# A graph network kernel: the radial and weight products of its second message stage read all 128 rows

## What is computed

```python
h = jax.nn.silu(radial_embedding @ W_r1 * RADIAL_DIM ** (-0.5))   # 8 radial values, W_r1 8 x 8
w = h @ W_r2 * RADIAL_DIM ** (-0.5)                               # W_r2 8 x 128
w_ss, w_vs, w_vt, w_st = jnp.split(w, 4, axis=1)
m_s = jnp.concatenate([ss * w_ss, m_s_tp * w_st], axis=1)
m_v = jnp.concatenate([vs * w_vs[:, :, None], m_v_tp * w_vt[:, :, None]], axis=1)
S = jax.ops.segment_sum(m_s, receivers, num_segments=n) * inv
V = jax.ops.segment_sum(m_v.reshape(m_v.shape[0], -1), receivers, num_segments=n) * inv
```

## Time and profile before

| | us |
|---|---|
| median of 3 runs | 19515.98 |
| lowest and highest run | 19462.58, 19540.44 |
| span of the profiled execution | 19527.8 |
| PE matmuls busy | 13705.4 (70%) |
| PE weight loads busy | 10208.8 (52%) |
| DVE busy | 11589.1 (59%) |
| POOL busy | 10499.0 (54%) |
| ACT busy | 4277.9 (22%) |
| first and last vy of edge2 start about | 12780, 15870 |

### The profile page before, as it was taken

The page is one execution under the profiler, slowest core; times in us unless marked ns, Lnnn a source line. Parts: engine busy times, 40 slices in busy tenths (PEclk is TensorE's granted clock), DMA queues, the critical chain, the costliest instruction groups (busy, mean ns, idle before and its releaser), DMA issues. The chain is left out here.

```text
span 19527.8 us, 364942 instructions
## 1 busy us (share of the span) xinstructions
PE 13705.4 (70%) x67902; PEld 10208.8 (52%) x67903; DVE 11589.1 (59%) x52990; ACT 4277.9 (22%) x11127; POOL 10499.0 (54%) x15826
## 2 busy tenths in 40 slices
PE   4467666766555557856888887689999974565555
PEld 2246666664333336745777766356666653333334
DVE  7778888885333336845665655267777754444443
ACT  7742222221111113422333332211111111000000
POOL 8878888886555553223555553045555522555560
PEclk9999999996555558978999999755555566555555
DMA  3011111111221115734555555011111110111121
GB/s 134 0 16 30 32 31 31 30 31 44 58 57 57 57 56 158 217 102 114 155 154 153 155 152 123 10 35 39 39 39 39 39 25 24 40 41 41 41 41 18
DMA packets 1925133, 1295.55 MB, mean 66 GB/s; under 512 B 1295114, under 2 KB 1679741, under 8 KB 1925096
## 3 DMA queue, kind: packets, MB, share of 16 engines
q1 hardware_dynamic: 1600808, 593.17, 13.5%
q0 software_dynamic: 324288, 701.98, 13.2%
HBM read 933.63 MB, written 367.36 MB: 67 GB/s over the span
## 5 line engine op out<-in xcount | busy, mean ns | idle before, releaser
L977 DVE TENSOR_TENSOR agg<-agg,edge_psA 128x256 f32 x4992 | 2078.2, 416 | 2042.1 <-issue 1567.3
L951 POOL DMA_INDIRECT edge_sv<-tab,edge_ix x1664 | 1569.1, 943 | 2169.6 <-DVE edge_ix L1332 1735.8
L951 POOL DMA_INDIRECT edge_xs<-tab,edge_ix x1664 | 1589.5, 955 | 1615.0 <-DVE edge_ix L1592 1141.0
L951 POOL DMA_INDIRECT edge_fs<-tab_a,edge_ix x1664 | 1573.0, 945 | 1634.7 <-DVE edge_ix L1044 1187.0
L1611 PE MATMUL edge_psA<-edge_oh,edge_xs 128*128 128x256 f32 x3328 | 1580.5, 626 | 1146.1 <-DVE agg L977 877.6
L610 POOL DMA_INDIRECT by_src<-send_row,send_pl x1664 | 1615.3, 971 | 1257.4 <-issue 1097.3
L662 PE MATMUL send_psX<-x_res,send_ohT 128*128 x3328 | 1315.5, 499 | 1188.2 <-ACT send_ohT L643 1078.8
L460 POOL DMA_INDIRECT records<-place_pl,place_place x1568 | 1614.4, 1030 | 550.9 <-issue 515.4
L1611 PEld LDWEIGHTS edge_psA<-edge_oh,edge_xs 128*128 128x128 f32 x3328 | 922.3, 306 | 1803.8 <-issue 935.1
L662 PEld LDWEIGHTS send_psX<-x_res,send_ohT 128*128 128x128 f32 x3328 | 833.9, 311 | 1758.4 <-issue 1758.4
L1398 PE MATMUL edge_psA<-edge_oh,edge_m 128*128 128x128 f32 x6656 | 1593.2, 421 | 0.7 <-DVE edge_m L1367 0.7
(11 more groups left out here) (310 smaller groups left out, 31165.4 us busy)
## 6 DMA issues: line engine op xcount, KB each, us to landing
edge_fd<-tab_b SPq DMA_DIRECT2D x1664, 128.0 KB
max_row<-by_src SPq DMA_DIRECT2D x392, 258.0 KB
running<-max_back POOLq DMA_DIRECT2D x392, 256.0 KB
records<-count_tmpl SPq DMA_DIRECT2D x64, 858.0 KB
send_pl<-records SPq DMA_DIRECT2D x832, 66.0 KB
edge_pl<-records SPq DMA_DIRECT2D x832, 50.0 KB
place_pl<-in_edge_attr SPq DMA_DIRECT2D x781, 50.0 KB
by_src<-send_row,send_pl POOLq DMA_INDIRECT x1664
```

Of the source, the lines that this page charges most:

```text
L951: pool.indirect_dma_start(rows[b % len(rows)][:, k, :], None, table[:], bass.IndirectOffsetOnAxis(ap=ix[b][:, k:k + 1], axis=0)).then_inc( ...
L977: v.tensor_tensor(block, block, psA[b % 2][:, k * 2 * D:(k + 1) * 2 * D], ALU.add).then_inc((s_half if k == 0 else s_acc)[b], 1)
```

## The change

The two products read all 128 rows of their operands. `rT` and `hr` (two buffers each) are cleared once at the start of the stage by four memsets on DVE, and ACT and PE wait for these before their first step. ACT still writes only the 24 and 16 rows in use. `wr1` and `wr2` were cleared over all rows before. So the rows below hold zeros in both operands and add nothing to the sums. No other instruction is added, removed or moved; every engine's order in the stage is the same.

```diff
--- before.py
+++ after.py
@@ -1285,7 +1285,7 @@
         psR = [ph.bank(f"psR{k}") for k in range(2)]
         psW = [ph.bank(f"psW{k}") for k in range(2)]
         psA = [ph.bank(f"psA{k}") for k in range(2)]
-        s_w, s_turn, s_zero, s_c, s_go = (ph.sem(n) for n in ("s_w", "s_turn", "s_zero", "s_c", "s_go"))
+        s_w, s_turn, s_zero, s_c, s_go, s_rows = (ph.sem(n) for n in ("s_w", "s_turn", "s_zero", "s_c", "s_go", "s_rows"))
         s_half, s_acc = ph.sems("s_half", DEEP), ph.sems("s_acc", DEEP)
         s_rec, s_ix, s_got, s_oh = (ph.sems(n, DEEP) for n in ("s_rec", "s_ix", "s_got", "s_oh"))
         s_T, s_TT, s_R, s_hr, s_W, s_m, s_C = (ph.sems(n, DEEP) for n in ("s_T", "s_TT", "s_R", "s_hr", "s_W", "s_m", "s_C"))
@@ -1315,6 +1315,8 @@
             v.memset(agg[:], 0.0).then_inc(s_zero, 1)
             v.memset(wr1[:], 0.0).then_inc(s_zero, 1)
             v.memset(wr2[:], 0.0).then_inc(s_zero, 1)
+            for t in (*rT, *hr):
+                v.memset(t[:], 0.0).then_inc(s_rows, 1)
             v.wait_ge(s_w, 32 * G2)
             w2 = wr2[0:8 * G2]
             v.tensor_scalar(w2, w2, 8 ** -0.5, None, ALU.mult).then_inc(s_zero, 1)
@@ -1369,6 +1371,8 @@
 
         @block.scalar
         def _(act):
+            act.wait_ge(s_rows, 4)
+
             def step(s, g, b, r):
                 o, n = two_before(b, r, DEEP)
                 if s == 0:
@@ -1385,6 +1389,7 @@
         @block.tensor
         def _(pe):
             pe.wait_ge(s_zero, 5)
+            pe.wait_ge(s_rows, 4)
 
             def step(s, g, b, r):
                 o, n = two_before(b, r, DEEP)
@@ -1401,13 +1406,13 @@
                 elif s == 1:
                     pe.wait_ge(s_hr[b], r + 1)
                     wait(pe, s_m[o], n)
-                    pe.matmul(psW[b % 2][:, 0:G2 * D], hr[b % 2][0:8 * G2, :], wr2[0:8 * G2].rearrange("p k c -> p (k c)"),
+                    pe.matmul(psW[b % 2][:, 0:G2 * D], hr[b % 2][:], wr2[:].rearrange("p k c -> p (k c)"),
                               start=True, stop=True).then_inc(s_W[b], 1)
                 elif s == 2:
                     pe.wait_ge(s_TT[b], r + 1)
                     wait(pe, s_hr[o], n)
                     pe.sem_inc(s_go, 1)
-                    pe.matmul(psR[b % 2][0:8 * G2, 0:P], wr1[0:G2 * RN].rearrange("p k c -> p (k c)"), rT[b % 2][0:G2 * RN, :], start=True,
+                    pe.matmul(psR[b % 2][0:8 * G2, 0:P], wr1[:].rearrange("p k c -> p (k c)"), rT[b % 2][:], start=True,
                               stop=True).then_inc(s_R[b], 1)
                 else:
                     pe.wait_ge(s_rec[b], (r + 1) * 16)
```

## The result

| | before | changed |
|---|---|---|
| median, 4 runs each, us | 19510.81 | 19215.82 |
| lowest to highest, us | 19462.58 to 19540.44 | 19181.33 to 19230.91 |
| span of the profiled execution, us | 19527.8 | 19223.7 |
| first to last `vy` of edge2, us | 3086.7 | 2803.0 |
| one turn of edge2 (that over 831), us | 3.71 | 3.37 |

The ratio is 0.986, with a 95% interval of 0.9837 to 0.9882: 295 us or 1.5% faster. The forecast was 19158; the time lies inside the range, some 58 us above the forecast. The two profiled spans differ by 304 us, and edge2 by 284 of these. The other 20 lie in the stage place (3397 us from its first to its last instruction before, 3377 after), which the change doesn't touch.

A forecast was written before the change was run, and what follows sets the result against it. PE at half clock was taken to bound edge2, then DVE's queue: 832 x (3.71 - 3.28) = 358 us off the profiled 19527.8 gives 19170, less 12 us to the runs' median 19158 us; range 19065 to 19330.

The forecast's parts named there:

- PE bounds edge2 at half clock: In edge2, PE is busy 3081 of 3090 us at clock 0.50 and sets the pace, 3.71 us a turn.
- The clock, by rows: In edge2, full rows raise PE's clock from 0.50 to near 1.0; its turn falls from 3.70 to 2.43 us or less.
- The rule of busy time: In edge2, busy time alone would already give 2.4 GHz and the change nothing; the forecast weighed rows used instead.
- The loads: In edge2, PE's weight loads start early, saving 0.31 and 0.07 us; 3.32 us a turn at half clock, 3.35 taken.
- rival B: In edge2 only the loads move, clock stays 0.50: some 3.40 us a turn, 258 us saved, 19258 us; chance 0.15.
- Rival C: In edge2 nothing changes, since a pass takes its columns' time whatever its rows: 19516 us; chance 0.15.
- What is late next: In edge2, DVE's own queue then sets the pace: 3.28 us a turn, bounds 3.17 and 3.70.
- Rival D: Edge2's DVE queue stumbles when nothing holds it back: 3.90 us a turn, 158 us more, 19674 us; chance 0.10.
- the sign that was named for D: DVE's block reads in edge2 reaching 700 ns and more.
- Other stages: All stages but edge2 keep their lengths within some 10 us.
- Others: In edge2, POOL's gathers need 2.48 us a turn, ACT 0.42, DMA is busy at 0.20; none becomes the bound.

The follow-up runs named there:

- split_few: The kernel before, with the second of edge2's two block reads a turn moved behind the second part of m: 18350.21 us, ratio 1.0.
- fill_r: Kernel before with the radial product on 128 rows and eight unread full-row transposes added a turn, weight product still on 16: 18052.44 us, ratio 0.983.
- w_only: The changed kernel with only the weight product (psW) on 128 rows, the radial product back on 24: 18062.05 us, ratio 0.9831 to before.
- r_only: The changed kernel with only the radial product (psR) on 128 rows, the weight product back on 16: 18379.93 us, ratio 1.0001 to before.
- rows64: The changed kernel with both products reading 64 rows in place of 128: 18381.6 us, ratio 1.0004 to before, a single run.
- rows96: The changed kernel with both products reading 96 rows in place of 128: 18044.18 us, ratio 0.982 to before, a single run.
- split_full: The changed kernel, with the second of edge2's two block reads a turn moved behind the second part of m: 17630.37 us, ratio 0.9609 to before.
- again: The changed kernel unaltered, run once more on another chip: 18034.35 us, ratio 0.9827 to before.

## Why the prediction was right, point by point

- **PE bounds edge2 at half clock.** Right: without PE's slowness the turn fell, and split_few shows that nothing on DVE mattered before.
- **The clock, by rows.** Right: 0.96 on the first chip. fill_r gives the whole gain by the clock alone. That it comes from rows was argued from edge1 against edge2, and w_only, r_only, rows64 and rows96 bear it out for rows or for what goes with them; the pauses at a change of rows stay a rival. PE's turn was put at 2.43 us or less, by the length of single passes; from psA to psT it is 1.85. That cost the forecast nothing, since DVE is behind both.
- **The rule of busy time.** The Trainium skill (TensorE: Matmul & The Clock Gate, Part 1) has sustained busy time release the throttle. The profile's busy row doesn't bear that out: PE at 3000 of 3000 us busy stays at 0.50 in r_only, and adding full-row passes to the same kernel gives 1.00.
- **The loads.** Right in kind for psW, wrong for psR and psT, whose loads are as late as before. The sum had 0.31 us from psW to psR and 0.07 from psR to psT; at half clock they are 0.16 and nothing, since 0.14 us of the step to psR is psR's own late load (0.56 us from the last pass of psW to psR, before and after). What the sum left out is the step into psW, 0.14 us shorter. Together 0.29 us against the 0.38 summed, and 3.42 us a turn against the 3.35 taken: so rival B, had it come, would have been worth some 240 us by this estimate, near the 258 foretold, in part by luck. The 0.42 us of the earlier trace rows is right for a pass with its load early; its second row, x3, is a burst of four cut off at the end of the window.
- **Rival C**, by the rule of the Trainium skill (TensorE: Matmul & The Clock Gate, LDWEIGHTS and Why this matters for your kernels) that the row count doesn't matter to a load or a single matmul. The runs agree for 16 and 64 rows (1.22 us for two passes at 0.50), not for 128, where the two take 1.06 us at the same clock as their loads start early; and the kernel's time changed, through the clock, of which the rule says nothing.
- **What is late next.** Right in kind: DVE's queue, shown by split_full. In size, 3.28 us was taken. In again the turn is 3.32: the common turn (3.17 to 3.22 foretold, 3.19 to 3.26 measured) and the branch turn (3.80, measured 3.81) were right, but two of eight turns take 3.35, which the three turns read in the earlier trace rows had not shown. That is (2 x 0.15)/8 = 0.04 us a turn, 31 us.
- **Rival D** came in a small part, on the first chip alone, and not by its block reads. There the turn is 3.37 against 3.32 in again, 44 us over the stage. What L965 runs on the DVE queue: its register operations before, changed and in again, then its block reads, changed and in again.

```profile
L965 DVEq FUSED_REGOPS  x2593: 57/190/190, 12900.2 to 15858.3; - x200
L965 DVEq FUSED_REGOPS  x2564: 2/190/715, 12900.7 to 15558.0; - x198
L965 DVEq FUSED_REGOPS  x2542: 57/190/190, 12300.4 to 14899.8; - x196
...
L965 DVEq TENSOR_LOAD <-blk x1581: 3/302/1421, 12900.4 to 15559.7; - x198
L965 DVEq TENSOR_LOAD <-blk x1565: 298/302/317, 12300.5 to 14899.4; - x196
```

  Laid beside again turn by turn, 805 of the 831 turns differ by 0.1 us in all; the 44 us stand in 26 turns. One is the third turn's `vy` at the start of the stage, 12.39 us after the second, where again has 3.42: 9 us, and no cost of the change, since the kernel before has such a wait there too (11.13 us). The other 25, worth 35 us, come in 16 bursts some 169 us apart. In and around them 47 instructions of the DVE queue take 0.4 us and more, mostly about 0.7, among them register operations, semaphore waits and asserts that otherwise take 0.02 to 0.19; only 9 are block reads, and these are 4.4 us longer than usual in all. So it is the queue as a whole that stumbles, and the sign that was named for D, long block reads, showed a tenth of it. Before, with PE in the way, edge2 had none on the same chip, as D says, and in again, on another chip, none takes 0.4 us; what causes them stays open. The two terms, 31 and 44, make up the 74 us by which edge2 was forecast too short: 358 us by the forecast, 284 measured. The total missed by less, 58 us, since 11 us of the gain between the medians lie outside edge2; that is luck.
- **Other stages** were to keep their lengths within some 10 us. Place is 20 us shorter in the one pair of profiles, which lies within the scatter of the runs (78 us between the lowest and the highest before).
- **Others.** POOL, ACT and the memsets cost nothing that shows, as said. By the forecast's estimate POOL's 2.48 us a turn would be next after split_full's 2.84.

## What to carry to other kernels

Where TensorE is busy without a gap and its granted clock is still low, look for matmuls that contract over few rows: zeros in the unused rows cost no pass time here and doubled the clock, and of two such products it was the one with more columns (256 against 128) that had to be filled. Before putting a number on it, find what the other engines' queues need for a turn, register reads and waits included, since busy shares hide them; then look there, for moving one register read to where the queue waits anyway gained more on top of the change (404 us) than the change itself (317 us on that chip), and nothing without it.

## What the runs showed that was not expected

Useless work made the kernel faster: eight more full-row transposes a turn took the kernel that had gained nothing (r_only, 18379.93 us, where the kernel before takes 18375.10) to 18052.44 (before on that chip: 18367.40).

Filling only psR did nothing, and 64 rows in both products did nothing; 96 gave nearly the clock of 128 (0.94 against 0.97).

The early start of psW's weight load came with 96 and 128 rows and not with 64; that of psR's, 16 columns wide, came with none (0.65 us idle ahead of it at half clock in r_only as before). Why is left open. The Trainium skill (TensorEngine Tiling, Key Properties) says that a change of tiling mode drains the array. psW's load agrees with it; psR's gap on 128 rows would need its few columns to count as a mode too. But then psT's load, 24 columns wide behind psR's 16, should be early, and it is late, while psA's, 128 columns wide behind psT's, is early in the kernel before. No run here varied the columns.

One chip gave 19511 us and three others 18352 to 18375 for the same kernel, with edge2 alike at half clock (3.71 us a turn). In edge3 the block reads of DVE reach 1404 ns on the first; in again, on another, none is over 322:

```profile
L965 DVEq TENSOR_LOAD <-blk x1664: 297/303/322, 15478.2 to 17596.6; - x185
```
